# Routing four groups of rows at a time in a fused StyleGAN-and-mixture-of-experts kernel on one Trainium2 core

## What is computed

```python
def _L0_cond_ref(x, style, weights, biases, mod_w, mod_b):
    out = x
    for i, typ in enumerate(('same', 'upsample', 'same', 'downsample')):
        out = _layer(out, style, weights[i], biases[i], mod_w[i], mod_b[i], typ)
    return out
def _L0_ffn_ref(hidden_states, gate_w, bias, Wg, Wu, Wd, Sg, Su, Sd):
    scores = jax.nn.sigmoid(x @ gate_w.T) + bias
    topk_w, topk_idx = jax.lax.top_k(scores, TOPK)          # TOPK = 4 of E = 16
    topk_w = topk_w / (jnp.sum(topk_w, axis=-1, keepdims=True) + 1e-20)
    cw = jnp.sum(jax.nn.one_hot(topk_idx, E) * topk_w[..., None], axis=1)
    z = jax.nn.silu(einsum('th,eih->eti', x, Wg)) * einsum('th,eih->eti', x, Wu)
    out = jnp.einsum('eti,ehi->th', z * cw.T[:, :, None], Wd)
    return out + jax.nn.silu(x @ Sg.T) * (x @ Su.T) @ Sd.T
return x + _L0_ffn_ref(_L0_cond_ref(x, ...), ...)
```

## Time and profile before

| | us |
|---|---|
| median of 3 runs | 1274.45 |
| lowest, highest | 1270.96, 1276.95 |
| the profiled execution | 1273.93 |
| its span (first to last instruction) | 1272.2 |
| TensorE clock granted over the span | 0.974 |

### The profile page before, as it was taken

How to read it: one execution, slowest core, us unless ns; L and a number is a source line. 1 busy time by engine, 2 the same in 40 slices (tenths; PEclk the granted TensorE clock), 3 DMA queues, 4 the chain that set the end, 5 groups by cost and what they waited for, 6 DMA issues and landing times. The chain is left out here.

```text
span 1272.2 us, 26362 instructions
## 1 busy us (share of the span) xinstructions
PE 1158.0 (91%) x7065; PEld 997.5 (78%) x7066; DVE 857.5 (67%) x2456; ACT 482.7 (38%) x1087; POOL 570.5 (45%) x844
## 2 busy tenths in 40 slices
PE   4698999999999999982999999999999999999995
PEld 3576777777777776761998999999998889999995
DVE  8387788887878887865565565655656665555653
ACT  4354444544555445431333232322324332222321
POOL 0021222222222222233566657666666566666764
PEclk9699999999999999995999999999999999999998
DMA  4356444444444444422666766676766767666664
GB/s 153 90 131 178 125 122 124 130 124 130 127 128 129 128 129 126 121 76 97 144 117 150 128 148 115 118 158 120 154 119 154 186 113 156 124 109 116 111 112 79
DMA packets 115059, 162.24 MB, mean 128 GB/s; under 512 B 22880, under 2 KB 72096, under 8 KB 113504
## 3 DMA queue, kind: packets, MB, share of 16 engines
q0 software_dynamic: 35616, 74.08, 32.2%
q1 hardware_dynamic: 78128, 87.93, 24.4%
q10 hardware_dynamic: 1296, 0.01, 0.1%
HBM read 73.28 MB, written 55.18 MB: 101 GB/s over the span
## 5 line engine op out<-in xcount | busy, mean ns | idle before, releaser
L388 POOL DMA_INDIRECT lists<-entry,place x128 | 134.0, 1047 | 432.1 <-DVE place L791 400.9
L1183 PE MATMUL bank<-xt_hi,wup_hi 128*128 128x256 f32 x1104 | 272.0, 281 | 2.3 <-ACT xt_hi L599 1.5
L1183 PE MATMUL bank<-xt_hi,wup_lo 128*128 128x256 f32 x1104 | 272.3, 280 | 0.0
L420 POOL DMA_INDIRECT out_rows<-yb,sid x140 | 227.3, 1624 | 85.2 <-DVE yb L964 57.7
L1183 PEld LDWEIGHTS bank<-xt_hi,wup_hi 128*128 128x128 f32 x1104 | 209.1, 189 | 7.3 <-issue 2.4
L1183 PEld LDWEIGHTS bank<-xt_hi,wup_lo 128*128 128x128 f32 x1104 | 208.2, 189 | 2.9
L406 POOL DMA_INDIRECT xg<-h_rows,gid x140 | 141.3, 1009 | 95.9 <-PE bank L1161 37.1
L1187 PE MATMUL bank<-xt_lo,wup_hi 128*128 128x256 f32 x1104 | 174.2, 280 | 0.0
L964 DVE TENSOR_SCALAR yb<-bank,all_lists 128x512 f32<-128x512 f32 x138 | 101.2, 749 | 107.5 <-DMA out_rows<-yb,sid 74.7
L202 PE MATMUL bank<-x_hi,cwt_hi 128*128 128x512 f32 (+1 forms) x352 | 139.9, 400 | 15.2 <-DVE x_hi L836 11.6
L507 ACT ACTIVATE t<-bank,cB,cA 128x256 f32<-128x256 f32 x256 | 127.3, 570 | 63.2 <-PE bank L209 53.9
(11 more groups left out here) (208 smaller groups left out, 2133.0 us busy)
## 6 DMA issues: line engine op xcount, KB each, us to landing
x<-x1p SPq DMA_DIRECT2D x256, 64.0 KB
x<-x1p SPq DMA_DIRECT2D x256, 63.8 KB
wraw<-in_Wup SPq DMA_DIRECT2D x11, 1024.0 KB
xraw<-in_x SPq DMA_DIRECT2D x32, 256.0 KB, 2.6
xbase<-in_x SPq DMA_DIRECT2D x32, 256.0 KB
h_rows<-hrow SPq DMA_DIRECT2D x128, 64.0 KB
out_rows<-orow SPq DMA_DIRECT2D x32, 256.0 KB
wdraw<-in_Wdn SPq DMA_DIRECT2D x11, 512.0 KB
```

Source lines behind the costliest of these rows:

```text
L388: pool.indirect_dma_start(out=lists, out_offset=bass.IndirectOffsetOnAxis(ap=place[:, par, k:k + 1], axis=0), in_=entry[:, par, k, :], in_ ...
L420: pool.indirect_dma_start(out=out, out_offset=bass.IndirectOffsetOnAxis(ap=sid[:, u, :], axis=0), in_=yb[:, u, :], in_offset=None, compute ...
L1183: pe.matmul(dst, lhs[a], rhs[0], start=k == 0 and a == 0, stop=False)
```

## The change

Routing is done for R = 4 groups together ("a round") in the groups 0 to 27, and one by one in the last four. The loop has four bodies a turn (bodies 4 to 27, `u` = 0 to 3), bodies 0 to 3 and 28 to 33 are written out.
- In every body DVE only reduces the logits of one group (one instruction) into its seat of `logit`.
- At u = 0 ACT takes the sigmoid of four groups and DVE runs `choose`; at u = 1 DVE runs `mark`. Both stand where the choice stood, ahead of `x0_lo`.
- At u = 2 PE does the prefix of four groups in 8 matmuls, and DVE runs `settle` behind `x1p` and ahead of `x2` (before, the places stood ahead of `xt_lo`).
- Body 28 runs `choose` and `mark` for the last round of four, body 29 its `settle`; bodies 29 to 32 do groups 28 to 31 singly, with `settle` in bodies 30 to 33.
- POOL puts the four groups of a round into the lists one after the other: the first at `place_ready`, the others behind the last `x3` of the same body, the last `x2` and the last `x3` of the next body.
- The edge correction is one instruction on 128 partitions instead of two on 32 (two more set-up instructions on DVE at the start). One store of zeros moves from SP to POOL.

```diff
+    R = 4
+    ROUNDS = G // R - 1
+    LAST = R * ROUNDS
...
+            with pool.Fori(0, ROUNDS - 1) as it:
+                pool.wait_ge(S["place_ready"], it + 1)
+                for r in range(R):
+                    if r:
+                        pool.wait_ge(S["x2_ready" if r == 2 else "x3_ready"], it * (4 * R) + 4 * (R + 2 + r // 2) + 4)
+                    scatter(2, r, "scattered")
...
+            def choose(number, many):
+                dve.wait_ge(S["sig_ready"], number)
+                step(dve.tensor_tensor(sc[:, 0:many], sig[:, 0:many], every(biasrow[:], many), ALU.add))
+                land(dve)
+                for r in range(many):
+                    ins = dve.max(top[:, r], sc[:, r])
+                step(ins)
+                dve.reduce_sum(tsum[:, 0:many], top[:, 0:many, 0:TOPK], AX_X)
+                for r in range(many):
+                    ins = dve.max_index(topi[:, r], top[:, r], sc[:, r])
+                step(ins)
+            def mark(home, scatters, many):
+                step(dve.tensor_copy(topf[:, 0:many], topi[:, 0:many, 0:TOPK]))
+                dve.tensor_scalar(tsum2[:, 0:many], tsum[:, 0:many], 1e-20, None, ALU.add)
+                step(dve.tensor_tensor(hot[:, 0:many].rearrange("p r k e -> p (r k) e"), every(iota_e[:], many * TOPK),
+                                       topf[:, 0:many].rearrange("p r (k a) -> p (r k) a", a=1).broadcast_to([P, many * TOPK, E]), ALU.is_equal))
+                dve.reciprocal(trec[:, 0:many], tsum2[:, 0:many])
...
+                    dve.reduce_sum(mask[:, 0:many], hot[:, 0:many].rearrange("p r k e -> p r e k"), AX_X).then_inc(S["mask_ready"], 1)
...
+            def settle(number, home, many):
+                dve.wait_ge(S["prefix_done"], number)
...
+                        step(dve.reduce_sum(msum[:], mask[:, 0:R].rearrange("p r e -> p e r"), AX_X))
+                        dve.tensor_tensor(mask[:, R, :], mask[:, R, :], msum[:], ALU.add)
...
+                step(dve.tensor_tensor(pos[:, 0:many], bank[7][:, 0:many * E].rearrange("p (r e) -> p r e", r=many),
+                                       every(region[:], many), ALU.add))
+                step(dve.tensor_tensor(hotpos[:, 0:many], hot[:, 0:many], across(pos[:, 0:many], TOPK), ALU.mult))
+                step(dve.reduce_sum(key[:, 0:many], hotpos[:, 0:many], AX_X))
...
                 if tail < 1:
                     layer0(g + 1)
+                if early and g > LAST:
+                    last = g - LAST
+                    settle(ROUNDS + last - 1, *((2, R) if last == 1 else (last % 2, 1)))
+                elif not early and u == 2:
+                    settle(it + 1, 2, R)
...
-                        for q, w in ((0, 0), (Q - 1, W - 1)):
-                            at = t2[C * q:C * q + C, two, w]
-                            r = dve.tensor_tensor(at, at, edge[C * q:C * q + C, bass.ds(g * NB + 2 * ph, 2)], ALU.add)
-                        step(r)
+                        ends = t2[:, two, 0:W:W - 1]
+                        step(dve.tensor_tensor(ends, ends, edge[:, bass.ds(g * NB + 2 * ph, 2), :], ALU.add))
...
+                if stage and early and g >= LAST:
+                    last = g - LAST
+                    choose(ROUNDS + last, 1 if last else R)
...
+                elif not early and u == 0:
+                    choose(it + 1, R)
+                elif not early and u == 1:
+                    mark(2, ("scattered", it * (16 * TOPK * R) + 16), R)
                 if tail < 1 and not (early and g == G - 2):
                     first_in(g + 2, par, None)
...
-                    pe.matmul(bank[7][:, 0:E], tri[:], mask[:], start=True, stop=False)
-                    pe.matmul(bank[7][:, 0:E], ones[:], cum[:, par, :], start=False, stop=True).then_inc(S["prefix_done"], 1)
+                    pe.matmul(bank[7][:, 0:many * E], tri[:], mask[:, 0:many], start=True, stop=False)
+                    for r in range(many):
+                        if r:
+                            pe.matmul(bank[7][:, r * E:many * E], ones[:], mask[:, 0:many - r], start=False, stop=False)
+                        ins = pe.matmul(bank[7][:, r * E:r * E + E], ones[:], mask[:, R], start=False, stop=r == many - 1)
+                    ins.then_inc(S["prefix_done"], 1)
```

More of the change, by code:

```diff
@@ L555, in body @@
                              t3[:, 2 * ph:2 * ph + 2, :], 2, S["t3_ready"])
-                if stage:
+                many = scored(g, u)
+                if many:
                     act.wait_ge(S["logit_ready"], g)
-                    if not (early and g == 1):
-                        act.wait_ge(S["mask_ready"], g - 1)
-                    act.activation(sig[:], logit[:], ACT.Sigmoid).then_inc(S["sig_ready"], 1)
+                    act.activation(sig[:, 0:many], logit[:, 0:many], ACT.Sigmoid).then_inc(S["sig_ready"], 1)
                 if tail < 2:
@@ L742, in _ @@
             dve.tensor_scalar(cB[:, 3, :], ones[:, 0:B], cbias[:, 3:4], None, ALU.mult)
[L744 removed]
+            for q, w in ((0, 0), (Q - 1, 1)):
+                rows = slice(C * q, C * q + C)
+                r = dve.tensor_scalar(edge[rows, :, w], s[rows, 2, :], cbias[rows, 1:2], -UPK[0], ALU.mult, ALU.mult)
+            link(r)
             dve.memset(tsum[:], 0.0).then_inc(S["scales_ready"], 1)
@@ L1034, in columns, with body @@
                 return [w[0:rows, m, :] for w in cwt], [data(a) for a in range(2)], True
-            def body(g, par, tail=0):
+            def body(g, it, u, tail=0):
                 early = isinstance(g, int)
                 stage = tail < 3 and not (early and g == 0)
+                par = u % 2
+                many, number = 0, None
+                if early and g > LAST:
+                    many, number = R if g == LAST + 1 else 1, ROUNDS + g - LAST - 1
+                elif not early and u == 2:
+                    many, number = R, it + 1
                 if tail < 1:
@@ L1104, in body @@
                     pe.wait_ge(S["z_ready"], g)
-                    if not (early and g == 1):
-                        pe.wait_ge(S["place_ready"], g - 1)
+                    if many:
+                        pe.wait_ge(S["place_ready"], number)
                     turn_z(0, bank[7]).then_inc(S["zt_t"], 1)
@@ L1137, in _ @@
             layer0(0)
-            for g in range(3):
-                body(g, g % 2)
-            with pe.Fori(0, (G - 6) // 2) as it:
-                body(it * 2 + 3, 1)
-                body(it * 2 + 4, 0)
-            body(G - 3, 1)
-            body(G - 2, 0)
-            body(G - 1, 1, tail=1)
-            body(G, 0, tail=2)
-            body(G + 1, 1, tail=3)
-            pe.wait_ge(S["place_ready"], G)
-            pe.matmul(bank[7][:, 0:E], ones[:], cum[:, G % 2, :], start=True, stop=True).then_inc(S["count_done"], 1)
+            for g in range(R):
+                body(g, None, g)
+            with pe.Fori(0, ROUNDS - 1) as it:
+                for u in range(R):
+                    body(it * R + (R + u), it, u)
+            for g in range(LAST, G + 2):
+                body(g, None, g, tail=max(0, g - G + 2))
+            pe.wait_ge(S["place_ready"], ROUNDS + R)
+            pe.matmul(bank[7][:, 0:E], ones[:], mask[:, R], start=True, stop=True).then_inc(S["count_done"], 1)
             def turn_in(j, u):
```

189 lines of the change are left out of this document (96 added, 93 removed).

## The result

| | before, us | changed, us | ratio, 95% interval |
|---|---|---|---|
| first comparison | 1274.47 (1270.96 to 1276.95) | 1300.89 (1299.72 to 1305.41) | 1.0206, 1.0182 to 1.0231 |
| the same two kernels in a later job | 1256.78 (1255.14 to 1260.35) | 1250.39 (1248.09 to 1251.39) | 0.9942, 0.9923 to 0.9961 |

The forecast of 1264.5 us (1257 to 1272) was wrong: in the comparison that it was made for, the change costs 2.1%. The experiments then brought a second fact that no profile of one job (one allotment of a chip, in which several kernels run after each other) can show. There are **two kinds of job**. In one, `before` has a median of 1273 to 1275 us, and in the other of 1256 to 1257. All executions of a job were of one kind, and chips 4 and 11 have each shown both, so it is not a property of a chip. The first comparison was of the slow kind.

A forecast was written before the change was run, and what follows sets the result against it. PE bounds the first stage (92% busy), idling mainly for x0_lo behind DVE's routing, 0.9 us a group. Terms 9.9 + 2.7 - 1.1 - 1.45 - 0.3 + 0.5 - 0.4 = 9.85 us off 1273.9 give 1264.1, forecast 1264.5 (1257 to 1272).

The forecast's parts named there:

- the paragraph on DMAs: Stack loads and POOL's list scatters: the stack keeps about 1.0 us spare, scatters only move; no cost in the sum.
- Rival C: List scatters collide with the stack's issues or landing in the loop; slower, 1282 us; chance 0.05.
- rival A: Layer 0's end: the next wait, on hrow, catches 0.3 to 0.4 of each freed 0.9 us; 1271 us; chance 0.22.
- the wait on L836: PE's wait for the high part of x3: a chain from layer 2 through ACT, staying near 0.35 us a group.
- x0_lo in three bodies of four: Layer 0's wait on x0_lo at u = 1 to 3: gone, gaining 0.9 us in each body.
- the pipelined end of my range: choose at u = 0: three more searches and index searches cost 0.7 us, a search 0.1, against 1.5 unpipelined.
- settle: Between x1p and x2 at u = 2: takes 2.3 us, a new PE wait of 1.3 us once in four bodies.
- D, the branch: The doubled loop's branch back waits 1 to 2 us a turn for instructions; 1270 to 1276 us; chance 0.05.
- up to body 1: Start: zeroing 256 elements and one more small DVE operation ahead of the first x1p lose 0.4 us.
- bodies 1 to 3: Written-out bodies without any routing: each gains 0.9 us at x0_lo, 2.7 us together.
- body 28 to the last count matmul: Written-out end: -1.1 body 28, -1.45 body 29, -0.3 body 30, +0.5 us from shorter logits in the last three bodies.
- the loop's terms: A round gains 3 x 0.9 + 0.4 - 1.3 - 0.15 = 1.65 us; six rounds in the loop: 9.9.

The follow-up runs named there:

- before_eight: The kernel before, with POOL waiting for the places of two groups and issuing their eight scatters in a row, 16 times; ordinary job: 1263.88 us, 1.0055.
- no_lists_3: The changed kernel without its 128 list scatters, second stage on padding rows, in a slow job: 1236.48 us.
- edge_only_2: The kernel before with only the new edge correction, in an ordinary job: 1257.19 us, 1.0001 of before.
- spaced_again: The changed kernel with the fourth group's scatters moved behind x1 of the next body, in the control's ordinary job: 1251.0 us, 0.9949.
- late_settle: The changed kernel with settle cut in two and the scatters placed anew, groups one and two making eight in a row; slow job: 1295.12 us, 1.0148.
- rounds_only: The changed kernel with the old edge correction (two instructions on 32 partitions), in a slow job: 1306.51 us, 1.0245 of before.
- edge_only: The kernel before with only the new edge correction, in a slow job: 1276.55 us, 0.9994 of before.

## Why the prediction was wrong

**The step that failed** is a clause of the paragraph on DMAs: "POOL's 128 indirect DMAs stay the same in number, and only their places move." I counted the scatters and asked with what they collide, but I didn't put the four starting points of a round on one time axis, and their new places entered the sum at nothing. The runs show that they cost this comparison eight stalls, 41 us of idle PE and a lowered clock behind each, 52.5 us against the same kernel in an ordinary job. In the trace of before, the last `x3` of a body follows its last `x2` by 5.5 us (261.77 to 267.24), and a group's four scatters take 5.2 (258.00 to 263.16). So two rows a few tenths of a microsecond apart could be read there, practically eight in a row. What they cost could not. Rival C put the loss at a collision with the `stack` and its price at 1282 us; nobody waited over 1.6 us for a `stack` in the loop. The sign was its, the mechanism and the size were not. "I would be wrong if layer 0's end waits for `hrow`" named the place exactly, and for another reason: rival A feared a delay of 0.1 us there.

**A second miss came before any sum.** In the earlier trace rows the wait on L836, 0.35 us a group, was laid to a chain from layer 2 through ACT, and kept as something that stays. The chain was right, and the wait is still the mark of the slow kind of job: 0.9 us in all in `before_eight`. What I didn't ask was why ACT is late in it. One such place of `before`, and the same place of `before_eight` in an ordinary job:

```profile
246.07 1.02 ACT L507 ACTIVATE t<-bank,cB,cA 128x256 f32<-128x256 f32 x2 [2.16 <-PE bank L209]
247.15 0.06 DVE L831 MEMSET t<- 64x2 f32 x1 [1.41 <-issue]
...
256.12 1.02 ACT L508 ACTIVATE t<-bank,cB,cA 128x256 f32<-128x256 f32 x2 [1.15 <-PE bank L209]
257.20 0.06 DVE L832 MEMSET t<- 64x2 f32 x1 [0.44 <-ACT t L508]
```

PE's half of layer 2 ended at 244.89 and at 255.86. ACT took it 1.18 us later in the slow job and 0.26 later in the ordinary one. DVE goes on 0.06 after ACT's pair in both. So the 19 to 24 us that the profile files on DVE under "issue", time in which an engine waits for nothing that the profile shows, are a wait for ACT there as well. They don't end with POOL's row: that ended at 246.34 here. What ties ACT's delay to the scatters is `no_lists_3`, where PE waits only 0.6 us in all for the high part of `x3`.

**What the sum got right.** The local terms are in the traces:
- *x0_lo in three bodies of four*: gone. At u = 0 0.5 us were to be lost. The changed kernel shows less:

```profile
256.21 0.41 DVE L811 MAX8 top<-sc 128x8 f32<-128x16 f32 x4 [0.15 <-DVE sc L808]
...
257.64 0.75 DVE L745 SCALAR_TENSOR_TENSOR x_lo<-xraw,own,x_hi 128x512 fp32r<-128x512 f32 x1 [0.23 <-DVE topi L815]
...
258.45 0.98 PE L213 MATMUL bank<-x_lo,cwt_hi 128*128 128x512 f32 x3 [0.16 <-DVE x_lo L745]
```

  Four searches take 0.41 us, 0.08 apart, so the pipelined end of my range held. The Trainium skill ("VectorE: DVE Perf Modes", section "The DRAIN you can't avoid") has the next operation wait until the pipe is empty, but adds that one which is not held starts earlier. My prediction used the first half alone; this trace bears out the second.
- *settle*: 2.3 us forecast, 2.37 measured (277.52 to 279.89), and the wait behind it 1.4.
- *D, the branch*: the Trainium skill ("Runtime: NRT & Kernel Launch", section "Instruction fetch mechanics") lets loops of this size fit; `no_lists_3`, with no wait of a turn, agrees.

**The sum in ordinary jobs.** I take `edge_only_2` as the stand-in for `before` there, since the two agree within 0.2%. PE's transposes of `hrow` stand at the same point of every body, here in body 5 and in body 28, first in `edge_only_2` and then in the changed kernel:

```profile
121.96 0.63 PE L1058 MATMUL bank<-ident,hrow 128*128 128x128 f32 x4
486.63 0.64 PE L1058 MATMUL bank<-ident,hrow 128*128 128x128 f32 x4
...
121.09 0.60 PE L1129 MATMUL bank<-ident,hrow 128*128 128x128 f32 x4
477.70 0.60 PE L1129 MATMUL bank<-ident,hrow 128*128 128x128 f32 x4
```

| stretch, by these transposes | forecast, us | measured, us |
|---|---|---|
| up to body 1 | -0.4 | +1.1 |
| bodies 1 to 3 | +2.7 | +2.1 |
| body 4, the first of the loop | +0.4 | -2.3 |
| bodies 5 to 27 | +9.5 | +8.1 |
| body 28 to the last count matmul | -2.35 | +0.4 |
| all of the first stage | 9.85 | 9.4 |

A turn of the loop gains 1.4 us (0.35 a body over 23 bodies), or 1.5 in its undisturbed middle, where the sum has 1.65. So the loop's terms, nearly all of the sum, had about the right size. Somewhat less than forecast arrives, as rival A said: the `x3` waits take 2.3 us in all, where `edge_only_2` has none. The rest agrees in part by luck. In body 4 PE waits 2.4 us for a `stack`; `spaced_again`, which differs in POOL's order alone, has no such wait, so it belongs to the execution. The start differs by 1.7 us between traces of ordinary jobs (57.7 and 56.0), more than the term put on it. The written-out end was forecast as a loss and is about even. Then 2.0 us are given back by a term that I didn't have. POOL is behind with its scatters, and the list load follows 9.1 us after the last count matmul instead of 7.1. 9.4 - 2.0 = 7.4 is about what the medians say, 6.4. It is no merit of the forecast that an ordinary job would have come near it: it was made from the trace of a slow job, for that job.

## What to carry to other kernels

When indirect DMAs are moved, write down when each row of them starts and ends, not only how many there are: two starting points closer than a row is long make a longer row, and what four in a row hardly show, eight may. Repeat the unchanged "after" beside every first experiment; without that control a variant in another job would have been taken for a repair. When a short wait recurs in every body, follow it back until an engine is late with its own condition met. And compare a gain over whole turns of a loop that lie inside it: a window that takes in the first written-out bodies behind it mixes two different things.

## What was unexpected of the hardware

The same program has two lives, job by job, and `before` showed both on each of two chips: it takes 1256 or 1274 us, the changed one 1250 or 1301, and without list scatters 1236.5 in a slow job and 1237 or 1244 in ordinary ones. In the slow kind, while POOL issues eight indirect scatters of 128 entries of 8 bytes (10.2 us), ACT and SP mostly stop for 3 to 6 us with their conditions met. SP goes on 1.1 us after POOL's last in the place shown. ACT goes on 1.3 to 2.3 after it behind fourteen rows of eight, those of the eight stalls of the first comparison and of the six in `late_settle`'s loop. But one row of eight in `rounds_only` holds ACT less, and in a row of sixteen it stops for 9 us and goes on before the row's end. Rows of four cost nothing that can be seen in `late_settle` and 0.7 us each in `edge_only`. PE's granted clock fell to its lower level at each of the eight stalls of the first comparison. The Trainium skill ("DMA: Bandwidth & Descriptors", section "SWDGE vs HWDGE vs iDMA") has the DMAs that POOL issues and those that SP issues in different queues of each engine, served in turn; that speaks of transfers. Here what stood still was the issue on SP and the compute on ACT, and the page doesn't tell why. What differs between the jobs, and through what the scatters reach ACT and SP, is not settled.
